# A Swin block on one core: q and k parts kept twice, the transfers in another order, gelu's high part by another instruction

## The reference

```python
y = _ln(x, norm1_g, norm1_b)
y = jnp.roll(y, (-SS, -SS), axis=(1, 2))          # then cut into B * 64 windows yw of 49 tokens
qkv = yw @ qkv_w.T + qkv_b
...
attn = jnp.einsum('bhqd,bhkd->bhqk', q * scale, k)
attn = attn + bias.transpose(2, 0, 1)[None]       # a table by relative position, and a mask at the edges
attn = jax.nn.softmax(attn.reshape(B * nW, HEADS, N, N), axis=-1)
o = jnp.einsum('bhqk,bhkd->bhqd', attn, v)
o = o @ proj_w.T + proj_b                         # windows back to images, rolled back
x = shortcut + o
h = _ln(x, norm2_g, norm2_b)
h = jax.nn.gelu(h @ fc1_w.T + fc1_b, approximate=False)
h = h @ fc2_w.T + fc2_b
return x + h
```

## Time and profile before

| | |
|---|---|
| time, median of 3 runs | 5146.63 us (5140.37 to 5152.69) |
| the profiled execution | 5130.69 us |
| its span | 5128.9 us |
| PE busy | 3941.8 us, 77% |
| DVE, ACT, POOL busy | 58%, 55%, 58% |
| mean granted clock of TensorE | 0.917 of full |
| DMA, mean | 87 GB/s |

### The profile page before, as it was taken

One profiled execution on the slowest core, in us unless ns is written; L12 is line 12 of the kernel. 1 busy time (PEld: TensorE's weight loads), 2 busy tenths in 40 slices (PEclk: granted clock), 3 DMA queues, 4 the chain that ended last, 5 costly groups with the idle time before them and its releaser, 6 DMA issues. The chain is left out here.

```text
span 5128.9 us, 216807 instructions
## 1 busy us (share of the span) xinstructions
PE 3941.8 (77%) x96144; PEld 3081.9 (60%) x96144; DVE 2974.2 (58%) x7839; ACT 2821.6 (55%) x3840; POOL 2995.4 (58%) x3983
## 2 busy tenths in 40 slices
PE   3777787777777787777777777778777877787777
PEld 2566666656666665665666666656666666666565
DVE  4555555556556555555555555555555555556564
ACT  1555555555555555555555555555555555555554
POOL 1566566566656656655655555566556555555665
PEclk9899989999999989999999989999999899899999
DMA  3443443444344344434433443444344334333432
GB/s 89 87 89 83 93 89 85 87 92 89 83 96 90 81 88 91 89 81 94 89 85 85 93 88 83 89 91 89 81 95 90 84 85 93 85 88 87 93 86 58
DMA packets 595395, 447.85 MB, mean 87 GB/s; under 512 B 125703, under 2 KB 594039, under 8 KB 594447
## 3 DMA queue, kind: packets, MB, share of 16 engines
q1 hardware_dynamic: 591979, 429.09, 38.9%
q10 hardware_dynamic: 2064, 3.21, 0.2%
q0 software_dynamic: 416, 1.68, 0.1%
HBM read 109.49 MB, written 51.46 MB: 31 GB/s over the span
## 5 line engine op out<-in xcount | busy, mean ns | idle before, releaser
L609 DVE TENSOR_REDUCE neg_max<-ps 113x16 f32<-113x784 f32 x1024 | 999.5, 976 | 723.7 <-PE ps L769 631.4
L430 ACT ACTIVATE probs<-ps,own 113x784 f32<-113x784 f32 x1024 | 917.7, 907 | 642.6 <-PE ps L801 586.0
L398 POOL TENSOR_TENSOR hid_lo<-probs,hid_hi 128x784 f16<-128x784 f32 x512 | 879.0, 1738 | 314.4 <-DVE hid_hi L603 314.4
L379 POOL TENSOR_SCALAR r_hi<-sums 128x98 f16<-128x98 f32 x128 | 175.2, 1368 | 1168.9 <-DVE sums L650 1168.9
L801 PE MATMUL ps<-st_q,st_k 127*49 127x49 f16 x32768 | 629.3, 186 | 130.6 <-issue 130.1
L801 PEld LDWEIGHTS ps<-st_q,st_k 127*49 127x49 f16 x32768 | 520.4, 103 | 216.7 <-issue 146.5
L492 ACT ACTIVATE k_hi<-ps,col 128x784 f16<-128x784 f32 x128 | 118.6, 926 | 927.8 <-DMA st_q<-q_lo 919.9
L769 PE MATMUL ps<-mx_k,mx_q 128*49 128x196 f16 x8192 | 546.1, 251 | 105.7 <-issue 43.8
L816 PE MATMUL ps<-probs,v_own 113*32 113x49 f32 x32768 | 515.1, 210 | 92.2 <-issue 61.3
L816 PEld LDWEIGHTS ps<-probs,v_own 113*32 113x32 f32 x32768 | 419.5, 110 | 206.2 <-issue 152.5
L848 PE MATMUL ps<-w_hi,hid_hi 128*112 128x128 f16 x3584 | 525.2, 226 | 12.9 <-issue 8.5
(11 more groups left out here) (112 smaller groups left out, 8710.0 us busy)
## 6 DMA issues: line engine op xcount, KB each, us to landing
st_k<-k_hi SPq DMA_DIRECT2D x256, 196.0 KB
st_q<-q_hi SPq DMA_DIRECT2D x256, 196.0 KB
oT_raw<-pv_sb SPq DMA_DIRECT2D x256, 196.0 KB, 6.0
x_in<-in_x SPq DMA_DIRECT2D x224, 196.0 KB
x_res<-in_x SPq DMA_DIRECT2D x224, 196.0 KB
out_y<-y_out SPq DMA_DIRECT2D x224, 196.0 KB
mx_k<-k_hi SPq DMA_DIRECT2D x512, 49.0 KB
mx_q<-q_hi SPq DMA_DIRECT2D x512, 49.0 KB
```

The lines of the kernel that those rows point to most:

```text
L379: nc.gpsimd.tensor_scalar(r_hi[:, :, :], sums[:, :, :], 1.0, 0.0, ALU.mult, ALU.add).then_inc(s_r_hi, 1)
L398: nc.gpsimd.tensor_tensor(hid_lo[:, c, :], hid[:, c, :], hid_hi[:, c, :], ALU.subtract).then_inc(s_hid_lo, 1)
L430: nc.scalar.activation(probs[0:KP, w % 4, :].rearrange("p (b c) -> p b c", b=2), ps[0:KP, b:b + 2, 0:HB * WT], ACT.Exp, scale=own[0:KP, 2: ...
L609: nc.vector.tensor_reduce(neg_max[0:KP, :, w].rearrange("p (g e) -> p g e", g=GQ), ps[0:KP, 0:2, :].rearrange("p b (g c) -> p (b g) c", g= ...
```

## The change

The q and k parts exist twice, one copy for odd and one for even steps, and ScalarE's wait before writing them is for the transfers of one step earlier. SP's order changes: two fills (the high rows of k and of q), sums, oT_raw, k's two cross fills, the row of maxima, r_rows, q's two cross fills, then mx_k and mx_q, out_y, x_res, and x_in last. The high part of gelu, a copy with a cast to fp16, becomes a tensor_reduce that takes the maximum over an innermost axis of one element, which gives the same values.

```diff
-        q_hi, q_lo, k_hi, k_lo = (sb(n, [C, NW, 2, WT], F16) for n in ("q_hi", "q_lo", "k_hi", "k_lo"))
+        q_hi, q_lo, k_hi, k_lo = ([sb(f"{n}{e}", [C, NW, 2, WT], F16) for e in range(2)]
+                                  for n in ("q_hi", "q_lo", "k_hi", "k_lo"))
...
                     sp.wait_ge(s_lo, 2 * (n + 1))
-                    fill(st_k, HIGH_ROWS, k_hi)
-                    fill(st_q, HIGH_ROWS, q_hi)
-                    fill(st_k, CROSS_ROWS[1], k_hi)
-                    fill(st_k, CROSS_ROWS[0], k_lo)
+                    fill(st_k, HIGH_ROWS, k_hi[odd(0)])
+                    fill(st_q, HIGH_ROWS, q_hi[odd(0)])
...
-                    band_dmas(sp, xr, x_in[odd(3)], n, edge(n), False, s_x)
-                n = t
-                if exists(n):
-                    fill(st_q, CROSS_ROWS[0], q_hi)
-                    fill(st_q, CROSS_ROWS[1], q_lo)
...
+                    fill(st_k, CROSS_ROWS[1], k_hi[odd(0)])
+                    fill(st_k, CROSS_ROWS[0], k_lo[odd(0)])
                     sp.wait_ge(s_negT, n + 1)
...
+                n = t
+                if exists(n):
+                    fill(st_q, CROSS_ROWS[0], q_hi[odd(0)])
+                    fill(st_q, CROSS_ROWS[1], q_lo[odd(0)])
...
+                n = t + 3
+                if exists(n):
+
+                    sp.wait_ge(s_st1, n)
+                    if past(n, 1):
+                        sp.wait_ge(s_t1, n - 1)
+                    band_dmas(sp, xr, x_in[odd(3)], n, edge(n), False, s_x)
...
-                    if past(n, 0):
-                        act.wait_ge(s_mx_dma, N_MX * n)
-                        act.wait_ge(s_st_dma, N_ST * n)
-                    for j, (hi, bank, b) in enumerate(((k_hi, 0, BK), (q_hi, 6, BQ))):
+                    if past(n, 1):
+                        act.wait_ge(s_mx_dma, N_MX * (n - 1))
+                        act.wait_ge(s_st_dma, N_ST * (n - 1))
+                    for j, (hi, bank, b) in enumerate(((k_hi[odd(1)], 0, BK), (q_hi[odd(1)], 6, BQ))):
...
-                nc.vector.tensor_copy(hid_hi[:, c, :], hid[:, c, :]).then_inc(s_hid_hi, 1)
+                nc.vector.tensor_reduce(hid_hi[:, c, :], hid[:, c, :].unsqueeze(2), AX_X, ALU.max).then_inc(s_hid_hi, 1)
```

More of the change, by code:

```diff
@@ L274, in body @@
                         sp.dma_start(sums[:, im, :], pv_sb[2 + im:C:32, :, :]).then_inc(s_sum_dma, 16)
-                n = t + 3
-                if exists(n):
-                    sp.wait_ge(s_st1, n)
-                    if past(n, 1):
-                        sp.wait_ge(s_t1, n - 1)
-                    band_dmas(sp, xr, x_in[odd(3)], n, edge(n), False, s_x)
-                n = t
-                if exists(n):
-                    fill(st_q, CROSS_ROWS[0], q_hi)
-                    fill(st_q, CROSS_ROWS[1], q_lo)
                 n = t - 1
@@ L314, in body @@
                         sp.dma_start(mx_k[32 * e:32 * (e + 1):4, :, e, :],
-                                     k_hi[e:C:EQ, :, :, :].rearrange("c w m q -> c (w m q)")).then_inc(s_mx_dma, 16)
+                                     k_hi[odd(1)][e:C:EQ, :, :, :].rearrange("c w m q -> c (w m q)")).then_inc(s_mx_dma, 16)
                     sp.wait_ge(s_hi, 2 * n + 2)
@@ L318, in body @@
                         sp.dma_start(mx_q[edge(n)][32 * e:32 * (e + 1):4, :, :],
-                                     q_hi[e:C:EQ, :, :, :].rearrange("c w m q -> c (w m q)")).then_inc(s_mx_dma, 16)
+                                     q_hi[odd(1)][e:C:EQ, :, :, :].rearrange("c w m q -> c (w m q)")).then_inc(s_mx_dma, 16)
                 n = t - 3
@@ L657, in body @@
                 if exists(n):
-                    for j, (hi, lo, bank, b) in enumerate(((k_hi, k_lo, 0, BK), (q_hi, q_lo, 6, BQ))):
+                    for j, (hi, lo, bank, b) in enumerate(((k_hi[odd(1)], k_lo[odd(1)], 0, BK), (q_hi[odd(1)], q_lo[odd(1)], 6, BQ))):
                         dve.wait_ge(s_hi, 2 * n + j + 1)
```

## The result

The changed kernel takes 4402.47 us in the median (4395.21 to 4410.66), beside 5149.15 for the kernel before on the same chip: ratio 0.8553, 95% interval [0.8533, 0.8572]. The two profiled spans, 5128.9 and 4399.1 us, differ by 730 us; 533 were predicted.

What follows compares the result with a forecast made beforehand. It took engines tied by transfers as the bound, chiefly ScalarE's wait before k_hi. Front 5.4 less clock 1.2 gave 4.2 us a step, x 127 = 533; 5130.69 - 533 = 4598, plus 16: 4614 us, range 4430 to 4850.

Steps and rivals of the forecast that it cites:

- what bounds the step: Whole step: engines tied by transfers, none busy throughout; largest wait ScalarE's before k_hi, 7.2 us a step.
- the first half of the chain: Front: k_hi at 6.7 us, the reciprocal of sums at 4.3, the q projection directly behind k at 6.7.
- the second rival: Front: sums lands no sooner because its own latency sets its time; 1.2 us a step gained, 4995 us; chance 0.08.
- The sign named for the first max_logits: Start of the loop: if the forecast is right, the first max_logits waits for mx_q.
- the reduce's price: gelu's high part on VectorE: a maximum over one element takes 0.98 us, a CAST 0.56.
- that it buys nothing: Front: r_lo ends 1.1 us earlier, but r_rows stands behind the k fills either way, so no gain from that alone.
- the slower rival: VectorE: a maximum is priced by its results; at 3.5 us each, 3.9 us a step lost, 5642 us; chance 0.05.
- the last transfers: End of the front: mx_k and mx_q cost two fills, landing at 17.2 us, when the first max_logits starts.
- the clock: Loop: TensorE's granted clock falls there, where there is no slack, costing 1.2 us a step, bounds 0 and 1.6.
- The rival "more": Whole step: clock stays up, mx_q early, x1 at 16.0 decides; 6.6 us a step gained, 4309 us; chance 0.05.
- Traffic does not slow the loop: Loop: x_in beside its first windows costs nothing; bounds nothing and 2.4 us a step.
- The second pair of maxima: VectorE ahead of x1: 0.84 us more than two casts, covered by mx_q coming 1.2 us later.

Runs made afterwards that it cites:

- four_fills: The changed kernel with k's two cross fills back ahead of sums, so that four fills stand in a row: 4907.52 us, ratio 0.9572.
- copies_only: The kernel before with two copies of the q and k parts and nothing else: 4955.18 us, ratio 0.9643.
- order_only: The kernel before with SP's new order of transfers alone, one copy of the parts and the cast kept: 5273.51 us, ratio 1.0266.
- cast_again: The changed kernel with the plain copy in place of all four maxima over one element, run a second time: 4374.82 us, ratio 0.8539.
- half_reduce: The changed kernel with the maximum kept in gelu's first pair and the plain copy in the second pair: 4352.45 us, ratio 0.8493.
- mx_q_on_act: The changed kernel with four plain copies, and mx_q's four transfers issued by ScalarE behind q_hi instead of by SP: 4525.38 us, ratio 0.8836.
- out_before_mx: The changed kernel with the stores of y_out issued ahead of mx_k and mx_q: 4585.24 us, ratio 0.8938.
- all_but_x: The changed kernel with the load of x_in back in its old place behind sums, ahead of oT_raw: 4655.63 us, ratio 0.9086.
- after_again: The changed kernel run once more, unaltered: 4393.33 us, ratio 0.8573.

## Why the prediction was wrong, step by step

**Right: what bounds the step, and the first half of the chain.** ScalarE's wait is gone, k_hi comes at 6.9 (6.7), the reciprocal at 4.23 (4.3), the q projection directly behind k at 6.68 (6.7). four_fills shows that two fills ahead of sums, and not sums's own latency, set that time, so the second rival falls; copies_only and order_only show that both parts are needed. L910 waits for r_rows as said, at 10.8 for 10.1. The sign named for the first max_logits, a wait for mx_q, came 47 times; 75 times it was x1.

**Right: the reduce's price. Wrong: that it buys nothing.** 964 ns (0.98 us), so the slower rival, by which its results set a higher price, did not occur; r_hi takes 287 ns (0.29) and r_lo ends at 6.2 (6.3). The Trainium skill, SBUF — State Buffer (SBUF: two separate sides), has a double-rate copy on VectorE and a GpSimd instruction shut each other out; the copy of 2.31 us beside x_b agrees. The prediction used that in one direction only, GpSimd held up by VectorE; in the new order r_hi starts free (319 ns in cast_again), and then r_lo is held by the first copy and the second copy by x_b. "r_rows stands behind the k fills whether r_lo ends at 6.3 or 7.4, so the edit on gelu buys nothing by that alone" holds for the packets of r_rows (L910 starts at 10.7 either way) and not for SP's queue: SP waits for r_lo, and mx stands behind. By half_reduce that is worth about 20 us.

**Failed first: the last transfers.** The step "mx_k and mx_q, 8 x 49 KB, as much as two fills, to 16.8, landed 17.2". q's fills land at 14.0 in the mean (13.6 predicted), and mx lands at 16.16, 2.1 us behind them where 3.6 was summed. The last of mx's packets ends at 15.7, 1.1 us sooner than summed. I costed them by bytes, as a fill carried by half of the engines. In the step shown, first 2.5 us of q's fills and then 1.5 us of mx, by their order in the queue:

```profile
1961.39:1963.89 2.50, 2.21 (x29) 1.85 (x30) 1.62 (x5) 2.46 (x4) 0.97 (x1) 1.00 0.55 97
1964.39:1965.89 1.50, 1.50 (x60) 1.37 (x60) 1.50 (x2) 0.71 (x1) 1.50 (x1) 1.00 0.56 201
```

The share of the DMA engines is the same, 0.55 and 0.56, and the rate is 201 GB/s where the fills have 97: mx costs about one fill and not two. Why its bytes go at twice the rate is open. SP's issues are a second bound close by: the eight ended at 14.3 in the mean (14.0 predicted), 1.4 us ahead of the last packet. That they alone set the time is not shown, and mx_q_on_act speaks against it. So mx_q and x1 (ended at 16.3, 16.0 predicted) arrive together, and max_logits starts at 16.63 and not at 17.2. Against the mean of before, 22.81, the front gave 6.18 where 5.4 was summed: 0.8 us a step, about 100 us; 0.2 of the 0.8 is that the step followed for the prediction began its loop at 22.61.

**Failed second: the clock.** The step "a fall would come in the loop, where there is no slack ... I take 1.2": a fall in each step, priced near the 1.6 of the row. Falls in the loop's first 2 us, behind the idle time ahead of max_logits, came in 7 steps of 116, and that idle time was 1.2 us and not 1.8. But had it been longer, the term would still have been too large: in out_before_mx it is 2.7 us, falls come at the loop's start in most steps, and they cost 0.3 us a loop. "No slack" is what was wrong. The other 34 falls of the kernel after begin later, and not behind a longer wait ahead of max_logits. The loop grew by 0.45 instead of 1.2: 0.75 a step, about 95 us. Loops without a fall grew by 0.1 of it (16.21 to 16.32).

Both errors together are 1.53 us a step, times 127 = 194, and 533 + 194 = 727. The rival "more", 4309, joined these two and had 0.05; what happened lies between it and the forecast. They are two errors and not one: with mx_q 1.5 us later, in out_before_mx, the loop was as long as in the kernel after (16.74 and 16.77). Both happened to lie on the same side, and together they left the range by 28 us.

**Small: x loaded last.** "Traffic does not slow the loop": 0.3 us a step by all_but_x, 0.1 against the kernel before. The second pair of maxima was to be covered by mx_q; of its 0.8 us a step 0.3 came through, the 41 us between half_reduce and after_again.

## What to carry to other kernels

Where two waits end at nearly the same place, do not judge a cure by its test alone: alone one of these gave 4% and the other lost 3%, and the whole change gave 14%. Follow a late transfer through every reader of its result, as sums here through y_out to the q projection and the mx transfers, before you price it. And before you price a fall of the clock, look at what TensorE has idle behind it to lose, and at how far behind it was before the fall: loops with a fall and loops without one differ in more than the clock.

## What the hardware showed that was not expected

- Four DMA issues on ScalarE held its next activation up by 3.05 us in the mean (381.7 us in 125 steps), 0.76 us each; on SP's queue four such issues take 2.55 us.
- A copy of 128 x 784 on VectorE took 1.92 us in the mean where it fell beside GpSimd's x_b and 0.56 to 0.70 elsewhere, and GpSimd's r_lo took 537 ns beside a copy and 285 beside a maximum; a maximum over one element with the same sizes took 0.96 to 0.97 us in either place.
- With TensorE at the lower clock at the loop's start, loops were 0.3 us longer (16.73 and 16.39). Where the fall came later they were 1.4 us longer, 0.95 of it before the fall.
- At the same share of the DMA engines, 0.55 and 0.56, q's fills moved 97 GB/s and the mx transfers 201.
- oT_raw landed 2.7 us after its issue in the median, and 6.0 before, now that x_in and four fills no longer stand ahead of it in the queue.
